# A float32 projection with routed low-rank adapters: the gate columns of batches 0 and 1 carried inside two output accumulators

## The chip, the cores and the metric

The kernel runs on one core of a Trainium2 chip. The metric is the device time of one execution in microseconds (us); lower is better. Five engines work side by side: TensorE (PE) multiplies matrices into PSUM, VectorE (DVE) and ScalarE (ACT) do elementwise work, GpSimd (POOL) does a few small elementwise steps here, and SyncE (SP) only issues DMAs. Each engine runs its own instructions in program order, and they wait for each other by counting semaphores.

## What is computed

For each of 8 batches of 256 rows and 1024 columns (float32), `adapter_ids` picks one of 8 weight matrices; the result y goes through `W_up`, and a rank-8 adapter, one of four chosen per row by a gate, is added; x is added last.

```python
y = einsum('bsi,boi->bso', x, weight[adapter_ids])      # first product
logits = y @ gate_w.T + expert_bias                      # 4 columns
one_hot = jax.nn.one_hot(jnp.argmax(logits, axis=-1), 4)
base_out = jnp.einsum('bth,oh->bto', y, W_up)            # second product
z = jnp.einsum('nh,erh->ner', y, lora_A)                 # 32 columns
d = jnp.einsum('ner,ehr->neh', z, lora_B)
out = x + base_out + jnp.einsum('neh,ne->nh', d, one_hot)
```

## The kernel before

**High and low parts.** A float32 operand is split in two fp32r tensors: a high part (a cast, by ACT) and a low part (the operand minus its high part, by DVE). A product is high times high, high times low and low times high, summed in PSUM.

**First product** (`first_product`, lines 785 and 787 on PE). Eight blocks of 128 output columns per batch, each 8 pairs of a 128x512 and a 128x256 matmul into one of two banks `ps_y`. For each block ACT copies the second half to `small`, and DVE adds it to the first half (`y_full`, line 562). Blocks of weights come by DMA into `w_raw`, and are split three blocks ahead (`w_hi_part` line 376 on ACT, `w_lo_part` line 517 on DVE). PE may start block n only when the sum of block n-2 is made.

**Second product.** y is held transposed in parts of four 128-deep slices: A11 and A12 are the two depth halves of rows 0 to 127 (t = 0), A21 and A22 those of rows 128 to 255 (t = 1). `W_up` is held in quarters B11, B12 (first depth half; output columns 0 to 511, 512 to 1023) and B21, B22. Batches 0 and 1 (`PLAIN = 2`) use `plain`: four accumulators (t, j), each a sum over 8 slices c of `term(t, j, c)`, which is `quarter`: three 128x512 matmuls (lines 803, 805, 807). Batches 2 to 7 use `strassen`: seven products of `quarter_wide` (line 796), which cuts each 512 columns into two halves over two banks, six matmuls per slice. In products 1 to 4 there the second half carries the gate columns too (GL = 36 columns: 32 of `lora_A` and 4 of `gate_w`), because these stand behind `W_up`'s columns in the tile `wide_hi`: 36 high ones and 36 low ones (`HALF + 2 * GL`). So the six matmuls of such a slice have 256, 328, 256, 256, 256 and 292 columns.

**Gates in batches 0 and 1.** `gates(b)` on PE (line 816) has 16 matmuls of their own, 72 gate columns as weights and 256 columns of y moving, after slice 5 of the first three accumulators. Their output lies transposed in `ps_p`; ACT and DVE add its halves and split it again (`g_parts`, `g_full`, `g_lo_part`), and `logits(b)` on PE (line 828, four small matmuls against `fold`) turns it back after slice 6. DVE's `choose` (lines 604 to 626) then adds the bias, finds the largest of four, masks z and writes `z_parts`; PE transposes those (line 835), ACT copies them to `zT` (line 408), and PE adds `zT` times `lora_B` (line 840, `add_lora`) to each accumulator. The transposes stand in the middle of accumulator (1, 1), the first three `add_lora` two slices later. DVE adds the finished accumulators to `rows` (line 580), and SP stores them.

**The gate columns' preparation.** SP loads `gl_raw` (line 306) behind all eight 512 KB units of `w_up` (`load_unit`, line 261). POOL computes a difference of two halves (line 351), ACT casts the four high parts in `constants` (line 415), POOL subtracts for the four low parts (line 355). The units of `w_up` are split by ACT (`unit_hi`, line 382) and DVE (`unit_lo`, line 524), units 0 to 2 during the last blocks of batch 0's first product and the others after it. PE waits for the first two gate parts (`gl_ready` 2) at the head of `gates(0)`.

Of the kernel before, what the change touches and what calls it, by code (L numbers as in the profile page):

```python
# [5 lines left out]
P = 128  # L6
# [19 lines left out]
def build(nc, xT, x, ids, w, w_up, gl, lora_b, bias, out):  # L26
# [51 lines left out]
    gates_before = [5 * max(b - PLAIN, 0) for b in range(B + 1)]  # L78
    products_before = [PARTS * max(b - PLAIN, 0) for b in range(B + 1)]

    with ExitStack() as ctx:
# [25 lines left out]
        wide_stage, wide_hi = sb_over("wide_stage", "wide_hi", [P, len(GATED), Q, HALF + 2 * GL])  # L107
        thin_stage, thin_hi = sb_over("thin_stage", "thin_hi", [P, PARTS - len(GATED), Q, HALF])
        up_raw, up_lo = sb_over("up_raw", "up_lo", [P, PARTS, Q, HALF])
# [14 lines left out]
        fold_f, fold = sb_over("fold_f", "fold", [P, GL])  # L124
        g_at = [place([P, T, P]) for _ in range(2)]
        g_hi = nc.alloc_sbuf_tensor_at("g_hi", [P, T, P], F32R, offset=g_at[0])
        g_kept = nc.alloc_sbuf_tensor_at("g_kept", [P, 2, 2 * GL], F32, offset=g_at[0])
        z_parts = nc.alloc_sbuf_tensor_at("z_parts", [P, T, P], F32R, offset=g_at[0])
        g_lo = nc.alloc_sbuf_tensor_at("g_lo", [P, T, P], F32R, offset=g_at[1])
        g_sum = nc.alloc_sbuf_tensor_at("g_sum", [P, T, 2 * GL], F32, offset=g_at[1])  # L130
# [6 lines left out]
        zg = nc.alloc_sbuf_tensor_at("zg", [P, T, GL], F32, offset=g_at[1] + T * 2 * GL * 4)  # L137
        zm = sb("zm", [P, T, ER])
        zT = sb("zT", [P, T, P], F32R)
# [9 lines left out]
        ps_plain = {(0, 0): ps_u[:, 0, :], (0, 1): ps_u[:, 1, :], (1, 0): ps_v[:, 0, :], (1, 1): ps_v[:, 1, :]}  # L149
        ps_g, ps_z = ps_p[:, 0, :], ps_p[:, 1, :]  # L150
# [4 lines left out]
        def gate_out(ps):  # L155
            return ps[:, 1, QUART:QUART + 2 * GL]
# [38 lines left out]
        g_done = sem("g_done")  # L195
        g_small_ready = sem("g_small_ready")
        g_full_ready = sem("g_full_ready")
        g_hi_ready = sem("g_hi_ready")
        g_ready = sem("g_ready")
# [18 lines left out]
        def gate_cols(q, ks, first=0, stop=2 * GL):  # L218
            return wide_hi[:, GATED.index(q), ks, HALF + first:HALF + stop]
# [19 lines left out]
        def _(sp):  # L239
# [19 lines left out]
            def load_unit(u):  # L259
                q, ks, (r, h, j) = quarter_of(u)  # L260
                sp.dma_start(up_raw[:, q, ks, :], w_up[r, h, j, :, :].rearrange("p (i n) -> p i n", i=2)
                             ).then_inc(up_raw_in[u], 16)
# [73 lines left out]
        def _(pool):  # L336
# [4 lines left out]
            pool.memset(fold_f[:, :], 0.0).then_inc(eye_step, 1)  # L341
            pool.wait_ge(eye_step, 3)
            pool.affine_select(out=fold_f[:, :], in_=fold_f[:, :], compare_op=ALU.not_equal, fill=1.0,
                               base=0, pattern=[[-1, GL]], channel_multiplier=1).then_inc(eye_step, 1)
            pool.wait_ge(eye_step, 4)
            pool.affine_select(out=fold_f[:, :], in_=fold_f[:, :], compare_op=ALU.not_equal, fill=1.0,
                               base=-GL, pattern=[[-1, GL]], channel_multiplier=1).then_inc(eye_step, 1)
# [5 lines left out]
            for n, (q, m) in enumerate(GATES):  # L353
                pool.wait_ge(gl_hi_ready, n + 1)
                pool.tensor_tensor(gate_cols(q, slice(0, Q), GL), gl_raw[:, m * Q:(m + 1) * Q, :],
                                   gate_cols(q, slice(0, Q), 0, GL).bitcast(F32), ALU.subtract).then_inc(gl_ready, 1)

        @block.scalar
        def _(act):
# [19 lines left out]
            def unit_hi(u):  # L379
                q, ks, _ = quarter_of(u)  # L380
                act.wait_ge(up_raw_in[u], 16)
                act.copy(up_hi(q, ks), up_raw[:, q, ks, :]).then_inc(up_hi_ready, 1)

            def t_hi(q):
                for j in range(2):
                    act.wait_ge(t_sum, t_sum_count(q, j))
                    act.copy(up_hi(q, pair(j)), up_raw[:, q, pair(j), :]).then_inc(t_hi_ready, 1)
# [8 lines left out]
            def g_parts(b):  # L396
                act.wait_ge(g_done, b + 1)
                act.copy(small[0:2 * GL, 0, :].rearrange("p (t n) -> p t n", t=T),
                         ps_g[0:2 * GL, :].rearrange("p (t j n) -> p t j n", t=T, j=2)[:, :, 1, :]
                         ).then_inc(g_small_ready, 1)  # L400
                act.wait_ge(g_full_ready, b + 1)
                act.copy(g_hi[0:2 * GL, :, :], small[0:2 * GL, 1, :].rearrange("p (t n) -> p t n", t=T)
                         ).then_inc(g_hi_ready, 1)

# [4 lines left out]

            def constants():  # L410
                act.wait_ge(gl_in, 16)
                for q, m in GATES:
                    if m == 2:
                        act.wait_ge(gl_sum, 1)
# [556 lines left out]
```

## Time and profile before

| what | us |
|---|---|
| median of 3 runs | 374.62 (374.54 to 375.24) |
| the profiled execution's own time | 374.81 |
| its span, first to last instruction | 373.0 |
| PE busy in the span | 367.5 (99%) |
| DVE, ACT, POOL busy | 262.4, 159.4, 6.6 |
| first product of batch 0 ends at | 31.26 |
| `plain(0)` on PE | 31.26 to 57.18 |
| granted TensorE clock, all 40 slices | 0.9 or more of full speed |

The span is 1.8 us shorter than the execution's own time. PE is busy almost without a gap, so the chain of waits runs almost wholly through PE, and its start times tell what a matmul costs in sequence: the distance between two starts, not the longer duration that a group of rows gives, since matmuls overlap.

### The profile page before, as it was taken

How to read it: one execution, taken by the hardware profiler on the slowest of the kernel's cores; microseconds unless marked ns; L12 is line 12 of the kernel's file. 1: busy time of each engine (PE TensorE's matmuls, PEld its weight loads, DVE VectorE, ACT ScalarE, POOL GpSimd, SP SyncE). 2: the span in 40 equal slices, each digit the busy share in tenths (PEclk: the TensorE clock that was granted, in tenths of full speed). 3: DMA queues.
4: the chain of work that ended last, by engine and by line, in shares of the span. 5: the costliest groups of instructions: out<-in, count | busy, mean ns of one | idle time of the engine just before them, and what ended most of it. 6: DMA issues, size and time to landing. Idle time of an engine off the chain costs nothing.

```text
span 373.0 us, 6260 instructions
## 1 busy us (share of the span) xinstructions
PE 367.5 (99%) x2348; PEld 334.7 (90%) x2348; DVE 262.4 (70%) x519; ACT 159.4 (43%) x320; POOL 6.6 (2%) x18
## 2 busy tenths in 40 slices
PE   7999999999999999999999999999999999999996
PEld 5888888888888999889998899989999899988996
DVE  4777587696758988678755786567874777746752
ACT  5667363642527543465115651155513553144300
POOL 1000500000000000000000000000000000000000
PEclk9999999999999999999999999999999999999999
DMA  7999975871069730687026760376404861160002
GB/s 244 402 394 312 408 286 182 325 226 57 0 192 340 252 119 0 226 302 243 21 96 210 270 216 3 147 250 231 163 2 178 324 213 76 49 234 0 2 1 114
DMA packets 19598, 68.19 MB, mean 183 GB/s; under 512 B 2288, under 2 KB 2416, under 8 KB 19568
## 3 DMA queue, kind: packets, MB, share of 16 engines
q1 hardware_dynamic: 19280, 66.74, 50.0%
q10 hardware_dynamic: 288, 1.05, 0.8%
q8 instruction: 19, 0.31, 0.3%
q14 instruction: 11, 0.09, 0.1%
HBM read 59.39 MB, written 8.39 MB: 182 GB/s over the span
## 4 chain that ended last, share of the span: by engine, by line
PE 97%; SPq 1%; DMA 1%; DVE 0%; issue 0%; ACT 0%; DVEq 0%
PE ps_y L785 31%; PE ps_u L796 19%; PE ps_y L787 16%; PE ps_v L796 10%; PE ps_p L796 5%; PE ps_u L803 2%; PE ps_v L803 2%; PE ps_u L807 2%; PE ps_v L805 2%; PE ps_u L805 2%; PE ps_v L807 2%; PE ps_p L816 1%; DMA w_raw<-w_dram 1%; SPq L241 1%; PE ps_p L847 0%; PE ps_v L847 0%
## 5 line engine op out<-in xcount | busy, mean ns | idle before, releaser
L785 PE MATMUL ps_y<-x_hilo,w_hi 128*128 128x512 f32 x512 | 178.3, 392 | 0.3 <-DVE w_lo L510 0.3
L787 PE MATMUL ps_y<-x_hilo,w_lo 128*128 128x256 f32 x512 | 143.2, 280 | 0.0
L785 PEld LDWEIGHTS ps_y<-x_hilo,w_hi 128*128 128x128 f32 x512 | 95.8, 187 | 22.1 <-DVE w_lo L510 0.8
L787 PEld LDWEIGHTS ps_y<-x_hilo,w_lo 128*128 128x128 f32 x512 | 96.7, 189 | 0.1
L517 DVE TENSOR_TENSOR w_lo<-w_raw,w_hi 128x512 fp32r<-128x512 f32 x126 | 81.3, 688 | 16.9 <-ACT w_hi L376 16.2
L376 ACT CAST w_hi<-w_raw 128x512 fp32r<-128x512 f32 x126 | 71.8, 624 | 3.4 <-DMA w_raw<-w_dram 3.3
L391 ACT COPY small<-ps_y 128x256 f32<-128x256 f32 x64 | 23.8, 372 | 107.2 <-PE ps_y L787 107.0
L562 DVE TENSOR_TENSOR y_raw<-ps_y,small 128x256 f32<-128x256 f32 x64 | 27.2, 425 | 47.1 <-ACT small L391 47.1
L796 PE MATMUL ps_u<-up_lo,y_parts 128*128 128x256 f32 x192 | 38.4, 281 | 0.0
L796 PE MATMUL ps_u<-wide_hi,y_parts 128*128 128x256 f32 x192 | 34.8, 293 | 0.0
L573 DVE TENSOR_TENSOR y_parts<-y_raw,y_parts 128x512 fp32r<-128x512 f32 x50 | 32.5, 687 | 1.3 <-ACT y_parts L394 0.9
L394 ACT CAST y_parts<-y_raw 128x512 fp32r<-128x512 f32 x50 | 28.8, 619 | 9.6 <-DVE y_raw L568 9.6
L796 PE MATMUL ps_u<-thin_hi,y_parts 128*128 128x256 f32 x192 | 32.8, 283 | 0.0
L796 PEld LDWEIGHTS ps_u<-up_lo,y_parts 128*128 128x128 f32 x192 | 31.1, 189 | 0.0
L408 ACT CAST zT<-ps_y 128x128 fp32r<-128x128 f32 x16 | 3.5, 269 | 63.8 <-PE ps_y L835 63.8
L796 PEld LDWEIGHTS ps_u<-wide_hi,y_parts 128*128 128x128 f32 x192 | 27.5, 188 | 0.2
L796 PEld LDWEIGHTS ps_u<-thin_hi,y_parts 128*128 128x128 f32 x192 | 27.3, 190 | 0.0
L580 DVE TENSOR_TENSOR rows<-ps_u,rows 128x512 f32<-128x512 f32 x28 | 19.0, 684 | 7.3 <-PE ps_u L796 7.2
L504 DVE TENSOR_TENSOR x_hilo<-x_raw,x_hilo 128x512 fp32r<-128x512 f32 x32 | 20.5, 685 | 3.6 <-ACT x_hilo L363 3.4
L363 ACT CAST x_hilo<-x_raw 128x512 fp32r<-128x512 f32 x32 | 17.9, 617 | 3.5 <-DMA x_raw<-xT_dram 3.1
L796 PE MATMUL ps_v<-up_lo,y_parts 128*128 128x256 f32 x96 | 19.2, 282 | 0.0
L796 PE MATMUL ps_v<-thin_hi,y_parts 128*128 128x256 f32 x96 | 17.6, 286 | 0.0
(108 smaller groups left out, 393.7 us busy)
## 6 DMA issues: line engine op xcount, KB each, us to landing
w_raw<-w_dram SPq DMA_DIRECT2D x64, 512.0 KB, 4.4
rows<-x_dram SPq DMA_DIRECT2D x16, 512.0 KB, 5.7
out_dram<-rows SPq DMA_DIRECT2D x15, 512.0 KB, 2.6
x_raw<-xT_dram SPq DMA_DIRECT2D x14, 512.0 KB, 5.0
up_raw<-w_up_dram SPq DMA_DIRECT2D x8, 512.0 KB, 12.4
wide_stage<-w_up_dram SPq DMA_DIRECT2D x4, 512.0 KB, 14.0
thin_stage<-w_up_dram SPq DMA_DIRECT2D x4, 512.0 KB, 9.4
x_raw<-xT_dram ACTq DMA_DIRECT2D x2, 512.0 KB, 4.2
```

Source lines behind the costliest of these rows:

```text
L363: act.copy(x_hilo[:, 0, ks, :], x_raw[:, 1, ks, :]).then_inc(x_hi_ready, 1)
L376: act.copy(w_hi[:, n % RING, part], w_raw[:, n % RAWS, part]).then_inc(w_hi_ready, QUARTERS // HALVES)
L391: act.copy(small[:, c % 2, :], ps_y[c % 2][:, S:2 * S]).then_inc(y_small_ready, 1)
L394: act.copy(y_parts[:, p, :, 0, :], y_raw[:, p, :, 1, :]).then_inc(y_hi_ready, 1)
L504: dve.tensor_tensor(x_hilo[:, 1, ks, :], x_raw[:, 1, ks, :], x_hilo[:, 0, ks, :].bitcast(F32), ALU.subtract).then_inc(x_ready, 1)
L517: dve.tensor_tensor(w_lo[:, n % RAWS, part], w_raw[:, n % RAWS, part], w_hi[:, n % RING, part].bitcast(F32), ALU.subtract).then_inc(w_read ...
L562: dve.tensor_tensor(y_raw[:, p:p + 2, c % Q, 1, :], ps_y[c % 2][:, 0:S].rearrange("p (t n) -> p t n", t=T), small[:, c % 2, :].rearrange(" ...
L573: dve.tensor_tensor(y_parts[:, p, :, 1, :], y_raw[:, p, :, 1, :], y_parts[:, p, :, 0, :].bitcast(F32), ALU.subtract).then_inc(y_ready, 1)
L580: dve.tensor_tensor(rows[:, t, part].rearrange("p (h n) -> p h n", h=2), ps, rows[:, t, part].rearrange("p (h n) -> p h n", h=2), ALU.add) ...
L785: pe.matmul(ps_y[c % 2][:, :], w_hi[:, n % RING, cols], x_hilo[:, :, k, :], start=(k == 0), stop=False)
L787: last = pe.matmul(ps_y[c % 2][:, S:2 * S], w_lo[:, n % RAWS, cols], x_hilo[:, 0, k, :], start=False, stop=(k == KC - 1))
L796: last = pe.matmul(ps[:, h, 0:end - h * QUART], y_parts[:, p, k, y, :], up_lo[:, q, k, cols] if up is None else up(q, k, cols), start=star ...
```

## The change

Batches 0 and 1 get their gate columns as batches 2 to 7 do. Accumulators (0, 0) and (1, 0) now lie over two banks each (`ps_u`, `ps_v`) and are computed by `quarter_wide` with 36 more columns; (0, 1) and (1, 1) take the two banks of `ps_p`. In `wide_hi` only the 36 high gate columns remain, and the low ones move behind the low parts of `W_up` in a new tile `wide_lo`; `up_raw` and `up_lo` are cut into `wide_raw`, `wide_lo`, `thin_raw`, `thin_lo` accordingly. `gates`, `logits`, `g_parts`, `g_full`, `g_lo_part` and `fold` are gone. In `plain` the third accumulator is now complete before (1, 1) starts; `z_done` is signalled there, and the transposes stand after six slices of (1, 1). All four `add_lora` stand at the end. The gate table is loaded before units 4 to 7; ACT casts its first two high parts in block 6 of batch 0, POOL makes the first two low parts before the difference, and PE waits for them at the head of `plain(0)`. In `strassen` DVE no longer adds the two 36-column halves (`g_sum`).

```diff
-        gates_before = [5 * max(b - PLAIN, 0) for b in range(B + 1)]
+        gates_before = [2 * min(b, PLAIN) + 4 * max(b - PLAIN, 0) for b in range(B + 1)]
...
-        ps_plain = {(0, 0): ps_u[:, 0, :], (0, 1): ps_u[:, 1, :], (1, 0): ps_v[:, 0, :], (1, 1): ps_v[:, 1, :]}
-        ps_g, ps_z = ps_p[:, 0, :], ps_p[:, 1, :]
+        ps_plain = {(0, 0): ps_u, (0, 1): ps_p[:, 0, :], (1, 0): ps_v, (1, 1): ps_p[:, 1, :]}
...
+            sp.dma_start(gl_raw[:, 0:2 * Q, :], gl[:, :, :]).then_inc(gl_in, 16)
             for u in range(4, UNITS):
                 load_unit(u)
-            sp.dma_start(gl_raw[:, 0:2 * Q, :], gl[:, :, :]).then_inc(gl_in, 16)
...
-            pool.wait_ge(gl_in, 16)
+            gate_low(0)
+            gate_low(1)
             pool.tensor_tensor(gl_raw[:, 2 * Q:3 * Q, :], gl_raw[:, Q:2 * Q, :], gl_raw[:, 0:Q, :], ALU.subtract
                                ).then_inc(gl_sum, 1)
+            gate_low(2)
+            gate_low(3)
...
+                    if (b, c) == (0, 6):
+                        act.wait_ge(gl_in, 16)
+                        gate_high(0)
+                        gate_high(1)
...
-                g_parts(b)
...
-                g_full(b)
-                g_lo_part(b)
                 for q in range(XQ):
                     x_lo(b + 1, q)
                 dve.wait_ge(z_done, b + 1)
-                choose(b, ps_z[:, 0:T * GL].rearrange("p (t n) -> p t n", t=T))
+                dve.tensor_copy(zg[:, 0, :], gate_out(ps_u)).then_inc(g_step, 1)
+                dve.tensor_copy(zg[:, 1, :], gate_out(ps_v)).then_inc(g_step, 1)
+                dve.wait_ge(g_step, gates_before[b] + 2)
+                choose(b)
...
-                for y, up, more in ((0, up_hi, 2 * GL), (0, None, 0), (1, up_hi, GL)):
+                for n, (y, up) in enumerate(((0, up_hi), (0, up_lo), (1, up_hi))):
                     for h in range(2):
-                        end = (h + 1) * QUART + (more if h == 1 and gated else 0)
+                        end = (h + 1) * QUART + (GL if h == 1 and gated else 0)
...
+                    if j == 0:
+                        return quarter_wide(ps_plain[t, j], left, right, c % Q, c == 0, False, True)
+                    return quarter(ps_plain[t, j], left, right, c % Q, c == 0, False)
+
+                if b == 0:
+                    pe.wait_ge(gl_ready, 2)
                 for c in range(OC):
...
+                    term(0, 1, c)
                     term(0, 0, c)
-                    term(0, 1, c)
-                    term(1, 0, c)
-                    if c == Q + 1:
-                        gates(b)
+                    last = term(1, 0, c)
+                last.then_inc(z_done, 1)
...
+                for c in range(OC):
                     if c == Q + 2:
-                        logits(b)
-                for c in range(Q):
+                        transpose_z(b)
                     term(1, 1, c)
-                transpose_z(b)
-                for c in range(Q, OC):
-                    term(1, 1, c)
-                    if c == Q + 1:
-                        if b == 0:
-                            pe.wait_ge(lb_ready, 1)
-                        add_lora(b, 0, 0, ps_plain[0, 0])
-                        add_lora(b, 0, 1, ps_plain[0, 1])
-                        add_lora(b, 1, 0, ps_plain[1, 0])
+                add_lora_wide(b, 0, 0, ps_plain[0, 0])
+                add_lora(b, 0, 1, ps_plain[0, 1])
+                add_lora_wide(b, 1, 0, ps_plain[1, 0])
                 add_lora(b, 1, 1, ps_plain[1, 1])
```

The order on PE in `plain(0)`, before, from slice 5 of accumulator (1, 0) to slice 6 of it and the small matmuls. `y_parts,wide_hi` are the gate matmuls, with y moving; the sizes are rows by moving columns.

```order
L807 MATMUL ps_v<-wide_hi,y_parts 128x512
L816 MATMUL ps_p<-y_parts,wide_hi 72x256 x16
L803 MATMUL ps_u<-wide_hi,y_parts 128x512
L805 MATMUL ps_u<-up_lo,y_parts 128x512
L807 MATMUL ps_u<-wide_hi,y_parts 128x512
```

And now, one slice of the first three accumulators (lines are those of the changed kernel).

```order
L784 MATMUL ps_p<-thin_lo,y_parts 128x512
L786 MATMUL ps_p<-thin_hi,y_parts 128x512
L776 MATMUL ps_u<-wide_hi,y_parts 128x256
L776 MATMUL ps_u<-wide_hi,y_parts 128x292
L776 MATMUL ps_u<-wide_lo,y_parts 128x256
L776 MATMUL ps_u<-wide_lo,y_parts 128x292
L776 MATMUL ps_u<-wide_hi,y_parts 128x256
L776 MATMUL ps_u<-wide_hi,y_parts 128x292
L776 MATMUL ps_v<-wide_hi,y_parts 128x256
```

The 16 separate matmuls are gone, and the slices of two accumulators have six narrower matmuls where they had three.

On PE at the end of `plain(0)`, before: what follows the transposes.

```order
L835 MATMUL ps_y<-eye,z_parts 128x128 x2
L803 MATMUL ps_v<-thin_hi,y_parts 128x512
L805 MATMUL ps_v<-up_lo,y_parts 128x512
...
L840 MATMUL ps_u<-lb_parts,zT 128x512 x2
L840 MATMUL ps_v<-lb_parts,zT 128x512
L803 MATMUL ps_v<-thin_hi,y_parts 128x512
```

And now, to the start of batch 1's first product.

```order
L792 MATMUL ps_y<-eye,z_parts 128x128 x2
L782 MATMUL ps_p<-thin_hi,y_parts 128x512
L784 MATMUL ps_p<-thin_lo,y_parts 128x512
...
L804 MATMUL ps_u<-lb_parts,zT 128x256 x2
L797 MATMUL ps_p<-lb_parts,zT 128x512
L804 MATMUL ps_v<-lb_parts,zT 128x256 x2
L797 MATMUL ps_p<-lb_parts,zT 128x512
L766 MATMUL ps_y<-x_hilo,w_hi 128x512
```

Two slices of (1, 1), six matmuls, stand between the transposes and the first adapter product in both; behind that product stood two more slices, and now there are none.

POOL's whole work on the gate table, before and then now, with what it waits for.

```order
L351 TENSOR_TENSOR gl_raw<-gl_raw 128x144 [waits gl_in]
L355 TENSOR_TENSOR wide_hi<-gl_raw,wide_hi 128x4x36 [waits gl_hi_ready] x4
```

```order
L346 TENSOR_TENSOR wide_lo<-gl_raw,wide_hi 128x4x36 [waits gl_hi_ready] x2
L351 TENSOR_TENSOR gl_raw<-gl_raw 128x144
L346 TENSOR_TENSOR wide_lo<-gl_raw,wide_hi 128x4x36 [waits gl_hi_ready] x2
```

Two of the low parts moved ahead of the difference, and they are now what PE waits for before its first matmul of `plain(0)`.

## Rows read from the trace of the kernel before

**Rows 1.** The page: busy time by engine, and the chain that ended last.

```profile
PE 367.5 (99%) x2348; PEld 334.7 (90%) x2348; DVE 262.4 (70%) x519; ACT 159.4 (43%) x320; POOL 6.6 (2%) x18
...
PE 97%; SPq 1%; DMA 1%; DVE 0%; issue 0%; ACT 0%; DVEq 0%
```

**Rows 2.** Waits of PE, beside the warm-up's: total us, times, longest.

```profile
PE ps_y L785 <- DVE w_lo L510: 0.3, 1, 0.3
```

**Rows 3.** The chain in order of time (start us, us, what), `plain(0)` and the end of it.

```profile
31.26 0.40 PE ps_u L803
31.66 0.23 PE ps_u L805
...
43.93 1.87 PE ps_p L816 x16
...
47.90 0.39 PE ps_p L828 x4
48.29 0.33 PE ps_u L803
...
53.24 0.17 PE ps_y L835 x2
...
54.85 0.47 PE ps_u L840 x2
...
57.18 0.24 PE ps_y L785
```

**Rows 4.** The same chain in batch 2's `strassen`: products 1, 5, an adapter product.

```profile
127.28 3.03 PE ps_u L796 x24
...
139.41 2.87 PE ps_u L796 x24
...
145.60 0.24 PE ps_p L847 x2
```

**Rows 5.** POOL in order of time: start, us, what; the four low parts.

```profile
38.69 2.42 POOL L355 TENSOR_TENSOR wide_hi<-gl_raw,wide_hi 128x144 fp32r<-128x144 f32 x1 [7.17 <-ACT wide_hi L415]
...
41.08 1.48 POOL L355 TENSOR_TENSOR wide_hi<-gl_raw,wide_hi 128x144 fp32r<-128x144 f32 x1
...
42.52 0.94 POOL L355 TENSOR_TENSOR wide_hi<-gl_raw,wide_hi 128x144 fp32r<-128x144 f32 x2
```

**Rows 6.** DVE in order of time, 29 to 42 us.

```profile
29.88 1.23 DVE L524 TENSOR_TENSOR up_lo<-up_raw,thin_hi 128x1024 fp32r<-128x1024 f32 x1 [0.52 <-ACT thin_hi L382]
31.70 0.43 DVE L562 TENSOR_TENSOR y_raw<-ps_y,small 128x256 f32<-128x256 f32 x1 [0.60 <-ACT small L391]
32.65 1.23 DVE L524 TENSOR_TENSOR up_lo<-up_raw,wide_hi 128x1024 fp32r<-128x1024 f32 x1 [0.52 <-ACT wide_hi L382]
...
40.79 1.41 DVE L556 TENSOR_TENSOR lb_parts<-lb_raw,lb_parts 64x1024 fp32r<-64x1024 f32 x1
```

**Rows 7.** ACT in order of time: `unit_hi(1)`, and the four high parts.

```profile
28.79 1.05 ACT L382 CAST thin_hi<-up_raw 128x1024 fp32r<-128x1024 f32 x1
...
38.30 0.95 ACT L415 CAST wide_hi<-gl_raw 128x144 fp32r<-128x144 f32 x4
```

**Rows 8.** SP in order of time, last weight block ahead of the gate table.

```profile
11.74 0.33 SPq L250 DMA_DIRECT2D w_raw<-w_dram  x1
```

**Rows 9.** DMA issues of 11.7 to 12 us: KB each, us to landing.

```profile
w_raw<-w_dram SPq DMA_DIRECT2D x1, 512.0 KB, 11.6
```

**Rows 10.** DVE in order of time: first and last step of `choose`.

```profile
50.06 0.16 DVE L604 TENSOR_TENSOR lg<-ps_p,bias_sb 128x8 f32<-128x8 f32 x1
...
51.91 0.36 DVE L626 TENSOR_TENSOR z_parts<-zm,z_parts 128x64 fp32r<-128x64 f32 x2
```

**Rows 11.** DVE in order of time, turn from batch 0 to batch 1.

```profile
54.39 2.50 DVE L517 TENSOR_TENSOR w_lo<-w_raw,w_hi 128x512 fp32r<-128x512 f32 x4 [0.92 <-ACT w_hi L376]
...
58.00 1.28 DVE L580 TENSOR_TENSOR rows<-ps_v,rows 128x512 f32<-128x512 f32 x2
60.40 0.42 DVE L562 TENSOR_TENSOR y_raw<-ps_y,small 128x256 f32<-128x256 f32 x1 [1.12 <-ACT small L391]
```

More of the change, by code:

```diff
@@ L123, in build @@
         eye_f, eye = sb_over("eye_f", "eye", [P, P])
[L124 to L130, printed above, removed]
+        g_kept = sb("g_kept", [P, 2, GL])
+        zg = sb("zg", [P, T, GL])
         lg = sb("lg", [P, T, E])
@@ L216, in up_stage, with up_lo, up_raw, gate_hi @@
             return (wide_stage[:, GATED.index(q), ks, 0:HALF] if q in GATED else thin_stage[:, THIN.index(q), ks, :])
[L218 to L219 removed]
+        def up_lo(q, ks, cols=slice(0, HALF)):
+            return wide_lo[:, GATED.index(q), ks, cols] if q in GATED else thin_lo[:, THIN.index(q), ks, cols]
+        def up_raw(q, ks):
+            return wide_raw[:, GATED.index(q), ks, 0:HALF] if q in GATED else thin_raw[:, THIN.index(q), ks, :]
+        def gate_hi(q):
+            return wide_hi[:, GATED.index(q), :, HALF:HALF + GL]
+        def gate_lo(q):
+            return wide_lo[:, GATED.index(q), :, HALF:HALF + GL]
         def quarter_of(u):
@@ L408, in z_back, with gate_high @@
                     act.copy(zT[:, t, :], ps_y[t][:, 0:P]).then_inc(zt_ready, 1)
+            def gate_high(n):
+                q, m = GATES[n]
+                act.copy(gate_hi(q), gl_raw[:, m * Q:(m + 1) * Q, :]).then_inc(gl_hi_ready, 1)
             def constants():
[L411 to L414, printed above, removed]
-                    act.copy(gate_cols(q, slice(0, Q), 0, GL), gl_raw[:, m * Q:(m + 1) * Q, :]).then_inc(gl_hi_ready, 1)
+                act.wait_ge(gl_sum, 1)
+                gate_high(2)
+                gate_high(3)
                 act.wait_ge(lb_in, 4 * 16)
                 act.copy(lb_parts[:, :], lb_raw[:, :]).then_inc(lb_hi_ready, 1)
-                act.wait_ge(eye_step, 5)
+                act.wait_ge(eye_step, 2)
                 act.copy(eye[:, :], eye_f[:, :]).then_inc(eye_ready, 1)
-                act.copy(fold[:, :], fold_f[:, :]).then_inc(eye_ready, 1)
             def first_product(b):
@@ L791, in quarter_wide @@
             def quarter_wide(ps, p, q, k, start, stop, gated):
-                for y, up, more in ((0, up_hi, 2 * GL), (0, None, 0), (1, up_hi, GL)):
+                for n, (y, up) in enumerate(((0, up_hi), (0, up_lo), (1, up_hi))):
                     for h in range(2):
-                        end = (h + 1) * QUART + (more if h == 1 and gated else 0)
-                        cols = slice(h * QUART, end)
+                        end = (h + 1) * QUART + (GL if h == 1 and gated else 0)
                         last = pe.matmul(ps[:, h, 0:end - h * QUART], y_parts[:, p, k, y, :],
-                                         up_lo[:, q, k, cols] if up is None else up(q, k, cols),
-                                         start=start and y == 0 and up is not None, stop=stop and y == 1,
-                                         skip_group_check=True)
+                                         up(q, k, slice(h * QUART, end)), start=start and n == 0,
+                                         stop=stop and n == 2, skip_group_check=True)
                 return last
@@ L804, in quarter @@
                           skip_group_check=True)
-                pe.matmul(ps, y_parts[:, p, k, 0, :], up_lo[:, q, k, :], start=False, stop=False,
+                pe.matmul(ps, y_parts[:, p, k, 0, :], up_lo(q, k), start=False, stop=False,
                           skip_group_check=True)
@@ L808, in quarter @@
                                  skip_group_check=True)
-            def gates(b):
-                if b == 0:
-                    pe.wait_ge(gl_ready, 2)
-                n = 0
-                for t, p, q in ((0, A11, B11), (0, A12, B21), (1, A21, B11), (1, A22, B21)):
-                    for k in range(Q):
-                        last = pe.matmul(ps_g[0:2 * GL, t * 2 * P:(t + 1) * 2 * P], gate_cols(q, k),
-                                         y_parts[:, p, k, :, :].rearrange("p j n -> p (j n)"),
-                                         start=(n == 0), stop=False, skip_group_check=True)
-                        n += 1
-                last.then_inc(g_done, 1)
-            def logits(b):
-                if b == 0:
-                    pe.wait_ge(eye_ready, 2)
-                pe.wait_ge(g_ready, b + 1)
-                for t in range(T):
-                    for part in (g_hi, g_lo):
-                        last = pe.matmul(ps_z[:, t * GL:(t + 1) * GL], part[0:2 * GL, t, :], fold[0:2 * GL, :],
-                                         start=(t == 0 and part is g_hi), stop=False, skip_group_check=True)
-                last.then_inc(z_done, 1)
             def transpose_z(b):
```

94 lines of the change are left out of this document (33 added, 61 removed).

## The prediction

> **What bounds the kernel now.** I read the page's busy times first: PE is busy 99% of the span, and the chain that ended last lies 97% on PE [rows 1]. Then the waits: beside its warm-up PE waits 0.3 us in all [rows 2]. So every matmul removed is time saved, every one added is paid, and no other engine matters until PE waits for it. What a matmul costs in sequence is read from the chain's start times. In `plain(0)` the first row lasts 0.40 instead of 0.23: about 0.17 us of it is a wait for DVE's low part of unit 1, which ends at 29.88 + 1.23 = 31.11 [rows 3, 6]. From 31.66 to 43.93 the chain holds 53 matmuls of 512 columns (18 accumulator slices, less the first matmul): 12.27 / 53 = 0.2315 us each [rows 3]. A product of `strassen` without gate columns is 24 matmuls of 256 in 2.87 us, one with gate columns 3.03 us [rows 4], so a gated slice of six costs 3.03 / 4 = 0.7575 us.
>
> **What goes from PE.** The 16 gate matmuls are one row, 1.87 us [rows 3]. The four `logits` matmuls take 0.39, and the matmul behind them 0.33 instead of 0.23: together 0.49 us [rows 3]. Both lie on the chain. Batch 1 has the same two groups, so 2 x (1.87 + 0.49) = 4.72 us go.
>
> **What comes on PE.** Per batch, 16 slices (8 of accumulator (0, 0), 8 of (1, 0)) turn from three matmuls of 512 into six of 256 and 292. A slice cost 3 x 0.2315 = 0.6945; it will cost what a gated slice of `strassen` costs, 0.7575, since the extra columns per slice are 3 x 36 = 108 in the new form and 72 + 36 = 108 in the one measured. The difference is 0.063, times 32 slices is 2.02 us. From below, if the gate columns were free, a slice would cost 2.87 / 4 = 0.7175 and the sum 0.74 us. From above, if each of the three wider matmuls cost what both wider ones of the measured slice do together (0.04), a slice would be 0.8375 and the sum 4.6 us, the whole gain. I take the measured form: the same six matmuls with the same number of columns, only spread otherwise. Two of four adapter products become two matmuls of 256 each: 0.24 for two [rows 4] against 0.47 / 2 = 0.235 for one [rows 3], 0.02 us for all four of them. In `strassen` nothing changes for PE: 72 + 0 + 36 extra columns become 36 + 36 + 36. Net on PE: -4.72 + 2.02 + 0.02 = -2.68 us.
>
> The Trainium skill (TensorE: Matmul & The Clock Gate, Back-to-back issue gap) gives 518 cycles for 512 columns and 262 for 256, and for 292 its formula N / 2.4 + 2.5 ns. The rows disagree: 0.2315 us and 0.1196 us (2.87 / 24), not 0.216 and 0.109. By the page, as an estimate, a slice would grow by 0.051 instead of 0.063 us and the change would save another 0.4 us; I go by the rows.
>
> **What is added in front of `plain(0)`.** PE now waits there for two low gate parts from POOL, ahead of all its work (the first term, (0, 1), has no gate columns but is queued behind the wait). Nothing hides this wait, since y and `W_up` are ready then. When do the parts come? The table's DMA: its issue now follows the last weight block of batch 0, issued at 11.74 and landed 11.6 us later, at 23.3 [rows 8, 9]; 144 KB behind 512 KB land within a microsecond, and ACT asks for them only at about 29.8. Units 4 to 7 come less than a microsecond later; ACT takes them only after units 2 and 3 and two parts of y, all behind 31.3, so they can spare it. ACT: its cast of unit 1 ends at 28.79 + 1.05 = 29.84; the two high parts follow, four of which took 0.95 us [rows 7], so they are ready near 30.1 and 30.3. Its next copy, for block 7, comes at 31.3 and is not delayed.
>
> POOL is the question. Undisturbed, a low part takes 0.47 us (two in 0.94), but the first took 2.42 and the second 1.48 [rows 5], while DVE ran splits of two SBUF tensors back to back until 42.20; the second ended 0.36 us after DVE did [rows 5, 6]. So such DVE work keeps POOL out. In the changed kernel POOL is ready at 30.1, inside DVE's split of unit 1 (29.88 to 31.11). I take the first low part as done 0.36 us after that, 31.47, and the second 0.47 later, near 31.95. DVE's step at 31.70 (`y_full`) reads PSUM and one SBUF tile, and I take it as harmless. PE then starts 0.32 us after that, as it did after DVE's 31.11 (31.43 against 31.11), so its extra wait is 31.95 - 31.11 = 0.84 us. From below: if POOL is not held up, 30.1 + 0.94 = 31.0, and the extra is 0. From above: if `y_full` (31.70 to 32.13) also holds it, 32.13 + 0.36 = 32.5, and the extra is 1.4 us. The rows are nearest to the middle, since the splits are the same form as those that did hold POOL.
>
> The Trainium skill (SBUF — State Buffer, Who interferes with whom) says that a DVE instruction with two SBUF inputs and a GpSimd instruction that reads SBUF exclude each other for a whole instruction, while a DVE instruction with at most one SBUF input does not contend. The trace agrees with the first half (2.42 us against 0.47). The second half is shown by no row here; by it the wait is 0.84 us, without it 1.4. This rule speaks against putting those steps in front of PE.
>
> **What must stay hidden.** (a) `choose`: DVE starts it when the first three accumulators are complete. From its first step to the end of its last, 50.06 to 52.27, are 2.2 us [rows 10], and two small copies out of PSUM come ahead, which I put at 0.4: 2.6 to 2.7 us. PE has six slices of (1, 1) before the transposes, 18 x 0.2315 = 4.2 us. Slack 1.5 us. (b) The transposes now stand 6 matmuls and four adapter products before the end, 2.5 us, where they stood 57.18 - 53.24 = 3.9 us [rows 3]. Behind them are queued ACT's casts and DVE's low parts of weight blocks 9 and 10, and behind those DVE's four row additions and `y_full` of the next batch's first block. Before, DVE's block of four low parts began 1.15 us after the transposes (54.39) and took 2.50 [rows 11]: now it ends 1.1 us after the batch's end. Four additions take 2 x 1.2 us [rows 11], to 3.6, and `y_full` is done at 4.0 instead of 60.82 - 57.18 = 3.6 us after the end. PE needs it two blocks in, at about 5.6 us. Slack 1.6 us. (c) ACT and DVE lose the whole `g_parts` loop, and DVE an addition of 36 columns in each `strassen`; they have idle time there, so that brings nothing.
>
> **The sum.** 374.81 - 2.68 + 0.84 = 372.97 for an execution like the profiled one (span 373.0 to 371.2). The profiled execution is 0.19 above the median, so against the median: 374.62 - 1.84 = 372.8 us, 0.5% faster.
>
> **Rivals.** First, **no extra wait**: POOL is not held up, because it gets its turn between two DVE steps. 374.62 - 2.68 = 371.9 us. For it: in rows 5 the first part ended at 41.11, before DVE's queue was empty. Against: 2.42 us. Chance 0.15. Second, **longer wait**: `y_full` holds POOL as well, 373.3 us; 0.15. Third, slower than before, **POOL is shut out**: if its second low part has not begun by 32.65, when DVE starts a run of splits without a gap [rows 6], it may get its turn only when that queue ends. In the trace the first was let in near 40.79, where its 2.42 us end at 41.11. The second part would then come near 41.1, the extra wait would be 41.1 - 31.11 = 10.0 us, and the time 381.9 us. It decides at 32.65, 0.7 us after my time for that part, and outweighs the gain once the part comes later than 31.11 + 2.68 = 33.8. Chance 0.05. Fourth, **cover used up**: the chain of `choose` or the turn to the next batch is longer than its slack of 1.5 us by up to a microsecond in each of two batches, or narrow slices cost more than in `strassen`: 373.5 to 375, about the time before; chance 0.10. It speaks against this that `strassen` runs the same slices with no wait, and that both slacks are large beside the steps that I guessed.
>
> **How the numbers follow.** My own case has 0.55, at 372.8. The range must hold 8 in 10: it reaches from the no-wait case to a little over the long wait, 371.8 to 373.7. A measurement of this kernel can tell about 0.2%, 0.75 us, from no change: faster means below 373.9. My case and the first two rivals are faster (0.85), with a fifth of the last, 0.02; the rest of the last gives 0.06 for the same and 0.02 slower, the shut-out another 0.05.
>
> **What would show it.** In the changed profile: first matmul of `plain(0)` near 32.3 with PE waiting for POOL's low part, and POOL's first two parts ending near 31.5 and 31.95; no rows of gate matmuls; a gated slice of `plain` at 0.76 us; `plain(0)` ending 0.5 us earlier than 57.18 and `plain(1)` shorter by 1.34; no wait of PE for `z_parts`, `zT` or `y_raw`. I am wrong if PE's wait exceeds 1.5 us, if slices cost 0.8, or if a wait appears at the turn of batches.

## The result

The changed kernel is not faster but a little slower: median 375.78 us against 375.11 us for the kernel before, 20 runs each, ratio 1.0024 (95% interval 1.0015 to 1.0034). I had forecast 372.8 us in a range of 371.8 to 373.7, so both the number and the sign are wrong. The profiled execution took 376.01 us, with a span of 374.2 us where it was 373.0.

The page first: PE is as busy as before, and its waits are the one that was forecast and the warm-up's.

```profile
span 374.2 us, 6363 instructions
...
PE 368.4 (98%) x2408; PEld 337.9 (90%) x2408; DVE 258.9 (69%) x513; ACT 158.0 (42%) x315; POOL 6.9 (2%) x15
```

```profile
PE ps_y L748 <- DVE warm L726: 2.0, 1, 2.0
PE ps_p L782 <- POOL wide_lo L346: 0.6, 1, 0.6
```

So PE has no new wait beside the one of 0.6 us. The chain in order of time shows that the part of the program that was changed did what was forecast. `plain(0)`, from POOL's two low parts over PE's first matmul and the last gated slice to the transposes and the next batch's first matmul (answers to [rows 3]):

```profile
30.66 1.77 POOL wide_lo L346 x2
...
32.47 0.50 PE ps_p L782
...
33.43 0.76 PE ps_u L776 x6
...
49.65 0.76 PE ps_v L776 x6
...
54.50 0.17 PE ps_y L792 x2
...
57.04 0.23 PE ps_y L766
```

A gated slice takes 0.76 us, and `plain(0)` ends at 57.04 where it ended at 57.18, although batch 0's first product ended 0.6 us later. The time went elsewhere, into work that the diff does not touch. Here are the first product of batch 3 and what follows it, in the chain of the kernel before and then of the changed one (start us, us, what):

```profile
149.20 0.23 PE ps_y L785
...
171.40 3.03 PE ps_u L796 x24
```

```profile
148.45 0.23 PE ps_y L766
...
171.06 3.04 PE ps_u L776 x24
```

The same 128 matmuls, with operands at the same places, took 171.40 - 149.20 = 22.20 us before and 171.06 - 148.45 = 22.61 us now. The page's groups say the same of all 512 long matmuls, before and after:

```profile
L785 PE MATMUL ps_y<-x_hilo,w_hi 128*128 128x512 f32 x512 | 178.3, 392 | 0.3 <-DVE w_lo L510 0.3
```

```profile
L766 PE MATMUL ps_y<-x_hilo,w_hi 128*128 128x512 f32 x512 | 181.2, 399 | 0.0
```

From the start times of the chains, phase by phase:

| phase | before, us | after, us | difference |
|---|---|---|---|
| start of the first product of batch 0 | 8.45 | 9.23 | +0.78 |
| from there to the end of batch 0's first product | 22.85 | 22.64 | -0.21 |
| from there to the end of `plain(0)` | 25.88 | 25.17 | -0.71 |
| first products of batches 1 to 7, each | 22.20 | 22.60 | 7 x 0.41 = +2.86 |
| `plain(1)` | 25.70 | 24.31 | -1.39 |
| `strassen`, six | 21.92 | 21.90 | -0.13 |

The sum is +1.2 us, the difference of the spans. The first row is the warm-up, whose 18 matmuls took 7.28 instead of 6.19 us: by the trace they start 427 ns apart thirteen times before the distance falls to about 230 ns, in the kernel before seven times. The windows of both profiles give the granted clock as 1.00 here, so they do not show the cause; the number of slow steps differs from run to run (6 to 11 in the variants below), and I count this row as chance. Without the two rows of batch 0's beginning, 2.86 - 2.23 = +0.63 us is left, and the medians differ by 0.67.

### The profile page after: what moved, and what is told of

The parts are those of the page before. It is cut to its first block, busy times and chain, and to the rows that moved or that the text cites. A ratio compares the mean times of both kernels' runs of the same rounds, so it can differ in the third digit from the quotient of the medians.

```text
span 374.2 us, 6363 instructions
## 1 busy us (share of the span) xinstructions
PE 368.4 (98%) x2408; PEld 337.9 (90%) x2408; DVE 258.9 (69%) x513; ACT 158.0 (42%) x315; POOL 6.9 (2%) x15
## 4 chain that ended last, share of the span: by engine, by line
PE 98%; POOL 0%; DVE 0%; ACT 0%; issue 0%; DVEq 0%
PE ps_y L766 32%; PE ps_u L776 22%; PE ps_y L768 16%; PE ps_v L776 13%; PE ps_p L776 5%; PE ps_p L782 2%; PE ps_p L784 2%; PE ps_p L786 2%; PE ps_y L748 2%; PE ps_v L804 1%; PE ps_u L804 1%; POOL wide_lo L346 0%; PE ps_p L804 0%; PE ps_y L797 0%; PE ps_y L792 0%; ACT thin_hi L380 0%
## 5 line engine op out<-in xcount | busy, mean ns | idle before, releaser
L766 PE MATMUL ps_y<-x_hilo,w_hi 128*128 128x512 f32 x512 | 181.2, 399 | 0.0
L776 PE MATMUL ps_u<-wide_hi,y_parts 128*128 128x256 f32 (+1 forms) x256 | 47.3, 289 | 0.0
L776 PEld LDWEIGHTS ps_u<-wide_hi,y_parts 128*128 128x128 f32 x256 | 39.5, 188 | 1.7
L776 PE MATMUL ps_v<-wide_hi,y_parts 128*128 128x256 f32 (+1 forms) x160 | 30.2, 289 | 0.0
L776 PE MATMUL ps_u<-wide_lo,y_parts 128*128 128x256 f32 (+1 forms) x128 | 26.5, 288 | 0.0
L776 PEld LDWEIGHTS ps_v<-wide_hi,y_parts 128*128 128x128 f32 x160 | 24.5, 188 | 0.0
L574 DVE TENSOR_TENSOR rows<-ps_u,rows 128x512 f32<-128x512 f32 x26 | 17.8, 683 | 7.6 <-PE ps_u L776 7.6
L776 PEld LDWEIGHTS ps_u<-wide_lo,y_parts 128*128 128x128 f32 x128 | 20.7, 188 | 0.0
```

The lines of the kernel that those rows point to most:

```text
L574: dve.tensor_tensor(row, ps, row, ALU.add).then_inc(row_step, 1)
L766: pe.matmul(ps_y[c % 2][:, :], w_hi[:, n % RING, cols], x_hilo[:, :, k, :], start=(k == 0), stop=False)
L776: last = pe.matmul(ps[:, h, 0:end - h * QUART], y_parts[:, p, k, y, :], up(q, k, slice(h * QUART, end)), start=start and n == 0, stop=stop ...
```

## What the first products do

The distance between the starts of one pair of matmuls (512 and 256 columns) and the next, in ns, tells more than the mean. In the kernel before it is 347, 346, 347 without end in batches 1 to 7, mean 346.7. In the changed one it is 350, 361, 349, again and again, mean 353.3. The work, the places of the tiles that these matmuls read and write and the granted clock (1.00 from 150 to 170 us) are the same in both. Batch 0 of the kernel before shows two patterns inside one product: pairs 6 to 15 run at 361, 349, 350, and behind one wait (distances of 486 and 451 ns) it goes at 343 and 350, mean 346.6. The wait is that of a weight load for DVE's `y_full`; PE's own list of waits does not have it:

```profile
14.35 0.19 PEld L785 LDWEIGHTS ps_y<-x_hilo,w_hi 128*128 128x128 f32 x1 [0.29 <-DVE y_raw L562]
```

So there are three patterns: flat (347, 346, 347) and alternating (343, 350), both fast with a mean near 346.7, and the slow one (350, 361, 349).

My theory (A): PE's stream of these matmuls can settle in more than one steady rhythm, and the state in which it is entered chooses which. The rival (B): something around it, as the position in the program or the traffic of the other engines, makes each matmul slower.

## Experiments

**The wait for POOL.** The changed kernel with the wait one term later:

```diff
-                if b == 0:
-                    pe.wait_ge(gl_ready, 2)
                 for c in range(OC):
...
                     term(0, 1, c)
+                    if b == 0 and c == 0:
+                        pe.wait_ge(gl_ready, 2)
                     term(0, 0, c)
```

> The changed kernel with one line moved: PE waits for the two low gate parts behind the first term of accumulator (0, 1), not ahead of it. That term is 3 matmuls of 512 columns, 0.69 us, against a wait of 0.6 to 0.8 us. If the wait is lost time on the chain, this kernel is 0.6 to 0.7 us faster than the changed kernel (375.1 where that has 375.8). If the wait is hidden in some other way, it is the same. In both cases the first products should still take 22.6 us each, if their slower rhythm has nothing to do with that wait; if the wait set it, they come back to 22.2 and the time falls by another 2.8 us.

Measured: 374.94 us, ratio to the kernel before 1.0001 (0.9992 to 1.0011), 0.8 us less than the changed kernel, and PE's wait for POOL is gone:

```profile
PE ps_y L748 <- DVE warm L726: 2.0, 1, 2.0
```

The first products of batches 1 to 7 stay at 22.6 us, so the wait did not set their rhythm.

**Disturbing the rhythm.** One extra matmul ahead of block 4 of each first product, with a size for each batch; its output is overwritten by the block's own first matmul.

```diff
+                        if b > 0 and c == 4 and k == 0:
+                            N = (0, 32, 64, 96, 128, 160, 192, 256)[b]
+                            pe.matmul(ps_y[c % 2][:, 0:N], w_hi[:, n % RING, cols], x_hilo[:, 0, k, 0:N],
+                                      start=True, stop=True)
```

> The changed kernel with one extra matmul in the middle of each first product of batches 1 to 7, ahead of block 4, of 32, 64, 96, 128, 160, 192 and 256 columns; its output is overwritten. Theory A: PE's stream of alternating 512 and 256 column matmuls can run in more than one stable rhythm (353.3 ns per pair in the changed kernel, 346.8 in the one before), and the state at entry chooses. Then some of the seven disturbances switch the second half of their product to near 346.8 ns and leave the first half at 353.3. Theory B: the slower rhythm comes from something around the stream (code position, traffic of other engines). Then both halves stay at 353.3 ns in all seven, and the time is that of the changed kernel plus 0.4 us for the extra matmuls.

Ns per pair, from the starts of the pairs in the trace, ahead of the disturbance (pairs 4 to 31) and behind it (pairs 36 to 63). The second kernel's rows belong to the next run:

| columns (batch) | 32 (1) | 64 (2) | 96 (3) | 128 (4) | 160 (5) | 192 (6) | 256 (7) |
|---|---|---|---|---|---|---|---|
| changed kernel, ahead | 353.3 | 353.3 | 353.3 | 353.3 | 353.3 | 353.3 | 353.3 |
| changed kernel, behind | 346.5 | 353.3 | 346.7 | 346.5 | 353.3 | 353.3 | 346.8 |
| kernel before, ahead | 346.7 | 346.7 | 346.7 | 346.7 | 346.7 | 346.7 | 346.7 |
| kernel before, behind | 346.7 | 346.5 | 346.6 | 353.3 | 353.3 | 346.7 | 346.8 |

PE in order of time in batch 3 of the changed kernel with the extra matmuls, around its 96 columns (start us, us, engine, line, shapes):

```profile
157.99 0.40 PE L770 MATMUL ps_y<-x_hilo,w_hi 128*128 128x512 f32 x1
...
158.35 0.40 PE L770 MATMUL ps_y<-x_hilo,w_hi 128*128 128x512 f32 x1
...
158.70 0.40 PE L770 MATMUL ps_y<-x_hilo,w_hi 128*128 128x512 f32 x1
...
159.05 0.40 PE L770 MATMUL ps_y<-x_hilo,w_hi 128*128 128x512 f32 x1
...
159.41 0.21 PE L768 MATMUL ps_y<-x_hilo,w_hi 128*128 128x96 f32 x1
159.46 0.46 PE L770 MATMUL ps_y<-x_hilo,w_hi 128*128 128x512 f32 x1
...
159.87 0.39 PE L770 MATMUL ps_y<-x_hilo,w_hi 128*128 128x512 f32 x1
...
160.22 0.39 PE L770 MATMUL ps_y<-x_hilo,w_hi 128*128 128x512 f32 x1
...
160.56 0.39 PE L770 MATMUL ps_y<-x_hilo,w_hi 128*128 128x512 f32 x1
...
160.91 0.39 PE L770 MATMUL ps_y<-x_hilo,w_hi 128*128 128x512 f32 x1
```

The long matmul's recorded 0.40 becomes 0.39, and the starts, 0.36, 0.35, 0.35 apart ahead of it, come 0.35, 0.34, 0.35 apart behind it; two digits hardly show the difference, and the table's means over 27 pairs do. Nothing but one small matmul stands between the two halves. One and the same product has both rhythms, and four sizes of seven switch it. The time, 375.80 us in one execution, is what the halves won less what the extra matmuls cost. Theory B falls.

> The kernel before with the same extra matmul ahead of block 4. Theory A: some of the seven second halves go from 346.8 to near 353.3 ns per pair. Theory B: all stay at 346.8.

In the kernel before, two sizes of seven throw a fast stream into the slow rhythm (last row of the table). Three others (64, 96 and 256 columns) turn the flat pattern into the alternating one, which the mean does not show. One execution: 376.34 us.

> As the run before, but the extra matmul stands ahead of block 0 of each first product. Theory A: in some batches the whole first product goes at near 346.8 ns per pair and takes 22.2 us plus the extra matmul, in others it stays at 353.3 and 22.6. Theory B: all stay at 353.3.

At the entry the same matmuls did little: only 32 columns in batch 1 gave 346.7 ns (its first product 22.31 us with the extra matmul), the other six stayed at 353. One execution: 376.05 us. So a disturbance is not a cure; it must hit right.

**Repeated disturbances**, with the late wait: 32 columns ahead of blocks 1, 2 and 3, or 96 ahead of blocks 1, 3 and 5.

> The changed kernel with the late wait of the first run, and one extra matmul of 32 columns ahead of blocks 1, 2 and 3 of each first product of batches 1 to 7 (0.03 us each, 0.55 us in all). One such disturbance took batch 1 from 353.3 to 346.5 ns per pair. Theory A: most products are in the fast rhythm by block 4, since a disturbance in the fast rhythm of that size left it (batch 1 of the kernel before), and the time falls from 374.9 to 372.9 to 373.5. If 32 columns work in batch 1 alone, the time is 375.3.

> As the run before, with 96 columns ahead of blocks 1, 3 and 5. In the scan 96 columns took batch 3 to the fast rhythm and left a fast batch fast. Theory A: all of batches 3 to 7 are fast from block 2 on, time near 373.8 (7 x 0.36 us less, 21 x 0.055 us more than 374.9). If the effect of one size depends on where in its period the stream is hit, some stay slow in block 1 and turn at block 3 or 5.

Both missed on the time: 375.03 and 375.60 us in one execution each. With 32 columns all seven products were fast from just behind the first extra matmul and stayed so behind the next two, so the rhythm did what was hoped; but each extra matmul took 0.11 to 0.12 us of the stream (in batch 3 ahead of block 3, distances of 375 and 433 ns in place of 347), not the 0.03 us expected, and three of them ate what was won, some 0.36 us: the products stayed at 22.6 us. With 96 columns, at 0.10 to 0.11 us each against 0.055 expected, batches 3 to 7 were flat behind block 1's, alternating behind block 3's and slow again behind block 5's, while batches 1 and 2 stayed slow throughout. So one size does not act alike everywhere: 96 columns ahead of block 1 meet batches 1 and 2 behind the distances 361, 349 and batches 3 to 7 behind 350, 350, another place in the same period.

**What chooses the entry.** The changed kernel has two kinds of difference ahead of a first product: other matmuls, and other places of tiles. The diff moved the small tiles behind `W_up`'s: by the sizes in the two kernels, `z_parts` now lies 864 bytes higher in each partition and `zT` 608 bytes lower. `zT` holds the weights of the adapter products. First, all small tiles back at their old places and no other change:

```diff
-        g_kept = sb("g_kept", [P, 2, GL])
-        zg = sb("zg", [P, T, GL])
+        place([P, GL])
+        g_at = [place([P, T, P]) for _ in range(2)]
+        g_kept = nc.alloc_sbuf_tensor_at("g_kept", [P, 2, GL], F32, offset=g_at[0])
+        z_parts = nc.alloc_sbuf_tensor_at("z_parts", [P, T, P], F32R, offset=g_at[0])
+        zg = nc.alloc_sbuf_tensor_at("zg", [P, T, GL], F32, offset=g_at[1] + T * 2 * GL * 4)
...
-        z_parts = sb("z_parts", [P, T, P], F32R)
```

> The changed kernel, with the small tiles behind W_up's (z_parts, zT, g_kept, zg and what follows) at the byte offsets that they had in the kernel before; the wide and thin tiles stay as changed. Theory A1: the entry state of the first products depends on where the operands of the last matmuls ahead lie, and zT is the weights of the adapter products. Then some or all of the products of batches 3 to 7 go back to 346.8 ns per pair, up to 0.41 us each. Theory A2: it is the width and order of the matmuls ahead that decides. Then all stay at 353.3 ns, and the time at 375.8.

Batch 3 in the chain:

```profile
148.38 0.23 PE ps_y L768
```

```profile
170.58 2.52 PE ps_u L778 x20
```

170.58 - 148.38 = 22.20 us, and so in all of batches 3 to 7; batches 1 and 2 stay at 22.61. One execution: 373.93 us. The opposite edit, the kernel before with these two tiles at the changed kernel's places (`g_hi`, `g_lo`, `fold` and other small tiles move with them):

```diff
+        g_at = [place([P, T, P]) for _ in range(2)][::-1]
+        zT = sb("zT", [P, T, P], F32R)
         fold_f, fold = sb_over("fold_f", "fold", [P, GL])
-        g_at = [place([P, T, P]) for _ in range(2)]
...
-        zT = sb("zT", [P, T, P], F32R)
```

> The kernel before, with z_parts and zT at the byte offsets of the changed kernel (the small tiles around them moved to make room), no instruction added, removed or moved in its order. If the place of these two tiles chooses the rhythm after a strassen batch, the first products of batches 3 to 7 take 22.6 instead of 22.2 us and the time is 5 x 0.41 = 2.0 us above the kernel before (377.0 where that has 375.0). If the place matters only together with the changed matmuls ahead, or with W_up's tiles, it is the time of the kernel before.

```profile
149.09 0.23 PE ps_y L785
```

```profile
171.71 3.04 PE ps_u L796 x24
```

171.71 - 149.09 = 22.62 us: batches 3 to 7 slow, 1 and 2 fast. Timed: 376.76 us, ratio to the kernel before 1.0044 (1.0028 to 1.0059). No instruction was added, taken away or moved, and the kernel before became slower than the changed one. The other placement test moved larger tiles:

> The kernel before with only the two tiles of W_up's high parts swapped in SBUF (thin ahead of wide), no instruction added, removed or moved. A1 (addresses take part): some phase changes its rhythm, in the first products (346.8 ns per pair becomes 353.3, 0.41 us each) or in the second products. A2 (only widths and order): every phase takes what it did, first products 22.20 us, strassen 21.92 us, plain 25.9 and 25.7.

All first products of batches 1 to 7 stayed at 22.20 us (375.21 us in one execution), so not every tile matters. Which of the two small ones does, in the changed kernel with the late wait:

```diff
+        place([P, 152])
         zT = sb("zT", [P, T, P], F32R)
```

> The changed kernel with the late wait, and only zT (the weights of the adapter products) at its old offset, by 608 bytes of padding; z_parts stays. If zT's place is what chooses, batches 3 to 7 take 22.2 us as with all tiles back; if it is z_parts (the weights of the transposes), they stay at 22.6; if the two together, either.

> The changed kernel with the late wait and 608 bytes of padding ahead of zT, timed. If zT's place alone brings batches 3 to 7 back, 374.94 - 5 x 0.41 = 372.9 us, and about 0.1 to 0.3 less if batch 0 is in its fast rhythm as in the look. If it was a chance of that execution, 374.9.

`zT` alone, 608 bytes of padding ahead of it: batches 3 to 7 at 22.20 us in both traces; 372.61 us in the first execution and 372.91 us as the median of five more, ratio 0.9936 (0.9923 to 0.9950), 2.0 us less than the late wait alone. Both runs are the same kernel, and the list of instructions is that of the late wait alone: only an address differs, so no difference in the position in the program or in the work of the other engines can be the cause. Batch 0's first product was fast in one (22.39 us) and slow in the other (22.73), behind waits of its own: there the rhythm changes from execution to execution.

> The changed kernel with the late wait and the small tiles at their old places. Batches 3 to 7 at 22.2 us, batches 1 and 2 at 22.6: 374.94 (late wait alone) - 5 x 0.41 = 372.9 us. If the look at the tiles' old places was a chance of one execution, 374.9.

With all small tiles back it is the same: 373.00 us, ratio 0.9944 (0.9928 to 0.9959).

**Batches 1 and 2** follow the plain batches and stayed slow in all of these variants of the changed kernel. The disturbance that had worked at the entry of batch 1 did not survive the move of the tiles:

> As the run before, with one extra matmul of 32 columns ahead of block 0 of batches 1 and 2. In the entry scan such a one cost under 0.1 us and took batch 1 from 22.60 to 22.28 us. Expected 372.9 - 2 x 0.32 = 372.2 us. Entry to these batches is not quite that of the scan (the tiles moved), so the kick may fail: then 373.0.

Measured 373.25 us, ratio 0.9953 (0.9941 to 0.9964); both products 22.69 us, slow, and longer by the extra matmul. Then the order of the last matmuls of `plain`, once with the transposes a slice earlier and one slice of (1, 1) put back behind the first three adapter products, and once with two adapter products swapped. DVE adds the accumulators in the order in which they are done, so the swap stands there too:

```diff
-                for i, (t, j) in enumerate(((0, 0), (0, 1), (1, 0), (1, 1))):
+                for i, (t, j) in enumerate(((0, 1), (0, 0), (1, 0), (1, 1))):
...
+                add_lora(b, 0, 1, ps_plain[0, 1])
                 add_lora_wide(b, 0, 0, ps_plain[0, 0])
-                add_lora(b, 0, 1, ps_plain[0, 1])
                 add_lora_wide(b, 1, 0, ps_plain[1, 0])
                 add_lora(b, 1, 1, ps_plain[1, 1])
```

> As e13's base (late wait, zT back), with the transposes one slice earlier and the first three adapter products ahead of the last slice of (1, 1), so that three matmuls of 512 columns and one adapter product of 512 stand last, as in the kernel before. If that tail is what gave the kernel before its fast batches 1 and 2, they take 22.20 us and the time is 371.8; PE must not wait for z_parts, since 15 matmuls of 0.227 us (3.4 us) cover 2.7 us. If the tail does not matter, 372.6 to 372.9.

> The changed kernel with the late wait and zT back, and at the end of a plain batch the adapter product of accumulator (0, 1) (one matmul of 512 columns) ahead of that of (0, 0) (two of 256). Same work. If the last matmuls choose the rhythm of the first product behind them, batches 1 and 2 may fall from 22.61 to 22.20 us (time 372.6 to 371.8); if they do not respond to so small a change, they stay at 22.61 and the time at 372.6 to 372.9.

The tail nearer to that of the kernel before missed: 373.20 us, ratio 0.9945 (0.9930 to 0.9960), batches 1 and 2 still at 22.61. The swap of two adapter products hit. Its chain, the last adapter products and the first product of batch 1:

```profile
55.74 0.24 PE ps_p L798
55.97 0.23 PE ps_u L805 x2
56.21 0.24 PE ps_v L805 x2
56.45 0.23 PE ps_p L798
56.68 0.23 PE ps_y L767
```

```profile
78.87 0.23 PE ps_p L783
```

78.87 - 56.68 = 22.19 us, and batch 2 the same; all seven products are fast (batches 1 and 2 in the alternating pattern, mean 346.7 ns, batches 3 to 7 in the flat one). Timed: 372.31 us, ratio 0.9919 (0.9904 to 0.9934). The two products give 0.84 us in the traces, the medians 0.6 us (five and four executions). Whether PE's new order or DVE's acts was not separated. This version, the changed kernel with one wait moved, 608 bytes of padding and the adapter products of two accumulators swapped, is 0.8% under the kernel before.

## Why the prediction was wrong

**The failed step** is in the sum, "374.81 - 2.68 + 0.84": it takes all that the diff does not touch as unchanged, a term of nothing for which the prediction gives no reason. I wrote that "in `strassen` nothing changes for PE", which was right (21.92 and 21.90 us), and never named the first products, whose seven times 22.20 us became 22.60. That term is +2.86 us, more than the whole gain. None of my rivals held it, and none of the signs that I had named for being wrong appeared. In the changed kernel 5 x 0.41 = 2.0 us of it come from the new place of `zT`: with it back the time falls from 374.94 to 372.91. The other 2 x 0.41 = 0.8 us, batches 1 and 2, do not answer to that place; swapping two adapter products removes them (372.91 to 372.31), but which of the diff's edits brought them was not found. The median of 3 that I started from lay 0.5 us under the later one of 20; from 375.11 the same sum gives 373.3, and that misses as well.

The kernel before had shown the signs. Batch 0's first product has two rhythms inside it. The mean of 0.2315 us that I took for a 512-column matmul is itself not a constant either: the changed kernel's chain of `plain(0)` has 18 of them between 50.41 and 54.50, 0.227 each. I read means where the distances were patterned.

**Point by point.**

- Gate matmuls and logits gone, gated slices: forecast -1.34 us per plain batch, measured -1.39 in `plain(1)` (24.31 against 25.70). The gated slice is 0.74 to 0.76 us in the chain, forecast 0.7575. The upper bound of 0.8375 did not come. (The estimate of another 0.4 us saved, which the sum did not use, was rounded on the way: its own figures give a growth of 0.0525 us per slice and 0.3 us.)
- The wait for POOL: forecast 0.84. POOL and DVE in order of time, as [rows 5, 6]:

```profile
30.66 1.31 POOL L346 TENSOR_TENSOR wide_lo<-gl_raw,wide_hi 128x144 fp32r<-128x144 f32 x1 [29.04 <-ACT wide_hi L401]
```

```profile
31.93 0.48 POOL L346 TENSOR_TENSOR wide_lo<-gl_raw,wide_hi 128x144 fp32r<-128x144 f32 x1
```

```profile
32.38 0.49 POOL L351 TENSOR_TENSOR gl_raw<-gl_raw 128x144 f32<-128x144 f32 x1
```

```profile
30.40 1.22 DVE L517 TENSOR_TENSOR thin_lo<-thin_raw,thin_hi 128x1024 fp32r<-128x1024 f32 x1 [0.53 <-ACT thin_hi L380]
32.28 0.42 DVE L555 TENSOR_TENSOR y_raw<-ps_y,small 128x256 f32<-128x256 f32 x1 [0.66 <-ACT small L389]
```

  DVE's split ended at 31.62; POOL's first part ended 0.35 us later (forecast 0.36), the second at 32.41, 0.79 after DVE. PE lost less than that, since its own first product ended later than in the kernel before (31.87 against 31.26): its wait is 0.6 us, and from the start of batch 0's last first-product matmul to the first of batch 1 the late wait takes 24.68 us where the changed kernel takes 25.32, 0.64 less. The medians differ by 0.8; the rest lies outside this stretch. The rule of the Trainium skill that the prediction weighed (SBUF — State Buffer, Who interferes with whom) agrees with this trace in both halves: 1.31 us beside a split of two SBUF tensors, and 0.48 and 0.49 for two POOL steps that overlap `y_full` at 32.28, which has one SBUF input.
- What had to stay hidden stayed hidden: PE waited for neither `z_parts` nor `zT` nor `y_raw`. `y_full` of the next batch's first block began at 60.46, 3.4 us after the batch's end, done at 3.8 (forecast 4.0, needed at 5.6):

```profile
60.46 0.41 DVE L555 TENSOR_TENSOR y_raw<-ps_y,small 128x256 f32<-128x256 f32 x1
```

- The rival of a POOL that is shut out did not happen; its second part began at 31.93, ahead of DVE's next split at 33.2.

What the changed part brings by itself, -0.71 - 1.39 - 0.13 = -2.2 us, is near the forecast of -1.84: the terms that I wrote down were right, and the one that I left at nothing took the gain. The 372.31 us of the last variant do not bear out my 372.8, since that variant has no wait for POOL; its own forecast is that of the rival without a wait, -2.68 us, which gives 372.6 from the 375.25 us that the kernel before took beside it.

## What to carry to other kernels

On an engine that is busy 99% of the time, compare the durations of the phases that a change does not touch before explaining anything by the ones that it does. In a stream of equal matmuls look at the distances between starts, not only at their mean: here a pattern of 350, 361, 349 beside a flat one of 347, 346, 347 was 2% of the stream, had or lost with no change in work. Such a gain or loss came here with the place of an unrelated tile and with the order of two small products, so measure an edit in more than one placement before judging it, and place the wait for a small side product behind the first work that does not need it.

## What the runs showed of the hardware

- The first product's stream ran in three patterns, flat and alternating (means of 346.5 to 346.8 ns per pair) and slow (353.3), in all seventeen traces, batch 0 included, with a mean granted clock of 0.998 to 1.0. In these traces a pattern lasts until something disturbs it: a wait (batch 0), or one matmul of another size.
- Ahead of block 4, extra matmuls of 32, 96, 128 and 256 columns switched the slow stream and 64, 160 and 192 did not; 128 and 160 threw the fast one into the slow rhythm. Each size was tried there in one batch. Ahead of block 1, 32 columns switched all seven batches and 96 only batches 3 to 7; at the entry only 32 in batch 1 worked. Each of 32 or 96 columns cost 0.10 to 0.12 us of the stream.
- Moving the tile of the adapter products' weights (1 KB in each partition) by 608 bytes moved the time by 2.0 us in the changed kernel. In the kernel before, the opposite move together with `z_parts` and other small tiles made it 1.7 us slower.
- What in the engine makes the rhythms stays open: in batches 1 to 7 no wait of PE and no difference in the granted clock goes with them. The first product does not read `zT`, and its rhythm still follows from `zT`'s place, so the state that the adapter products leave is what remains as the link; how the place of `zT` forms that state is not shown.
